# AdaLN block on one Trainium2 core: first batch's keys kept raw, scale in column blocks, keys and values by pairs, new engine orders

## What is computed

```
mod = (silu(c) @ wmod).reshape(4, 6, 1, 1024)          # sa, ca, ga, sb, cb, gb
ga, gb = sign * max(abs, 0.25)
h = layernorm(x) * (1 + ca) + sa
q, k, v = h @ Wqkv + bqkv                              # 3 x 256 columns
attn = softmax(q @ k.T / 16) @ v
x = x + ga * (attn @ Wo + bo)
h = layernorm(x) * (1 + cb) + sb
x = x + gb * (h @ weight.T + bias + LoRA(h))           # adapter by batch
```

## Time and profile before

| | us |
|---|---|
| median of 3 runs | 1043.1 (1042.88 to 1043.18) |
| the profiled execution | 1042.57, of which its span 1040.8 |
| PE busy | 1011.5 (97%) |
| VectorE busy | 663.6 (64%) |
| ScalarE busy | 309.2 (30%) |
| GpSimd busy | 231.2 (22%) |
| DMA | 180.74 MB, mean 174 GB/s |

### The profile page before, as it was taken

How to read it: one execution, slowest core, us unless ns; L and a number is a source line. 1 busy time by engine, 2 the same in 40 slices (tenths; PEclk the granted TensorE clock), 3 DMA queues, 4 the chain that set the end, 5 groups by cost and what they waited for, 6 DMA issues and landing times.

```text
span 1040.8 us, 12891 instructions
## 1 busy us (share of the span) xinstructions
PE 1011.5 (97%) x5158; PEld 831.6 (80%) x5158; DVE 663.6 (64%) x827; ACT 309.2 (30%) x460; POOL 231.2 (22%) x182
## 2 busy tenths in 40 slices
...
PEclk9899999999999999999999999999999999999999
...
GB/s 348 409 317 244 211 295 140 252 227 265 70 1 77 207 197 127 1 94 157 155 162 117 41 142 225 203 220 184 200 202 126 216 145 202 140 225 122 142 76 66
DMA packets 54475, 180.74 MB, mean 174 GB/s; under 512 B 5784, under 2 KB 6352, under 8 KB 54416
## 3 DMA queue, kind: packets, MB, share of 16 engines
...
q10 hardware_dynamic: 160, 0.53, 0.1%
...
## 4 chain that ended last, share of the span: by engine, by line
PE 91%; DMA 4%; DVE 2%; SPq 1%; issue 1%; POOL 0%; ACT 0%; DVEq 0%; POOLq 0%; ACTq 0%
PE pairC L1370 8%; PE pairA L1370 8%; PE pairC L1371 8%; PE pairC L1372 7%; PE pairA L1371 7%; PE pairA L1372 7%; PE pairD L1370 7%; PE pairD L1371 7%; PE pairD L1372 7%; PE pairB L1370 5%; PE pairB L1371 5%; PE pairB L1372 5%; DMA z_cols<-in_x_cols 2%; PE pairB L1526 1%; PE pairD L1478 1%; PE pairA L1478 1%
## 5 line engine op out<-in xcount | busy, mean ns | idle before, releaser
L923 POOL TENSOR_TENSOR xr<-xr,row_bc 128x1024 f32<-128x1024 f32 x32 | 79.9, 2503 | 110.1 <-DMA xr<-in_x 90.3
L936 POOL TENSOR_TENSOR res<-res,row_bc 128x1024 f32<-128x1024 f32 x32 | 81.7, 2565 | 83.4 <-DMA res<-x_dram 76.9
L1370 PE MATMUL pairC<-w_hi,h_hi 128*128 128x512 f32 (+1 forms) x256 | 90.1, 352 | 0.0
L1371 PE MATMUL pairC<-w_lo,h_hi 128*128 128x512 f32 (+1 forms) x256 | 90.0, 351 | 0.0
L1372 PE MATMUL pairC<-w_hi,h_lo 128*128 128x512 f32 (+1 forms) x256 | 89.6, 350 | 0.0
L1370 PE MATMUL pairD<-w_hi,h_hi 128*128 128x512 f32 (+1 forms) x224 | 77.6, 346 | 0.0
L1371 PE MATMUL pairD<-w_lo,h_hi 128*128 128x512 f32 (+1 forms) x224 | 77.6, 346 | 0.0
L1372 PE MATMUL pairD<-w_hi,h_lo 128*128 128x512 f32 (+1 forms) x224 | 77.2, 345 | 0.0
...
L1079 ACT ACTIVATE w_hi<-w_sum 128x1024 fp32r<-128x1024 f32 x32 | 33.8, 1059 | 100.5 <-DVE w_sum L1320 100.2
L1370 PE MATMUL pairB<-w_hi,h_hi 128*128 128x512 f32 (+1 forms) x160 | 59.8, 374 | 0.0
L1371 PE MATMUL pairB<-w_lo,h_hi 128*128 128x512 f32 (+1 forms) x160 | 59.3, 371 | 0.0
...
## 6 DMA issues: line engine op xcount, KB each, us to landing
wm<-in_wmod SPq DMA_DIRECT2D x48, 512.0 KB, 6.4
xr<-in_x SPq DMA_DIRECT2D x34, 512.0 KB, 4.0
z_cols<-in_x_cols SPq DMA_DIRECT2D x32, 512.0 KB, 6.3
x_dram<-xr POOLq DMA_DIRECT2D x32, 512.0 KB, 3.8
xs<-x_dram SPq DMA_DIRECT2D x32, 512.0 KB, 4.7
w2t<-in_w2t SPq DMA_DIRECT2D x32, 512.0 KB, 4.3
res<-x_dram SPq DMA_DIRECT2D x32, 512.0 KB, 5.7
out_y<-res POOLq DMA_DIRECT2D x31, 512.0 KB, 3.5
```

The lines of the kernel that those rows point to most:

```text
L923: nc.gpsimd.tensor_tensor(xt, xt, row_bc[:, :], ALU.add).then_inc(residual_made, 1)
L936: nc.gpsimd.tensor_tensor(rt, rt, row, ALU.add).then_inc(residual2_made, 1)
L1370: nc.tensor.matmul(out, left[0], right[0], start=first, stop=False)
L1371: nc.tensor.matmul(out, left[0], right[1], start=False, stop=False)
```

## The change

Everything in it is in the first batch, but for the five orders, which are new throughout.

- The scale (s = 0) is made in four blocks of 256 columns. A buffer now holds 256 columns of 512 rows of `wmod` (four pieces of 1 KB per partition where there was one of 4 KB), `M0(c)` multiplies two buffers, `MC0`, `MT0` and `MM0` finish two column tiles each, and `HH(0,0,k)` waits for block k alone.
- Mean and 1/deviation are spread apart (`BCM`, `BCP`), for both blocks of rows, and ScalarE copies them from PSUM to `bc` (`BMC`, `BPC`), from where `Z` reads. The way through DRAM is gone for block (0,1).
- `V0(c)` makes the first block's values two column tiles at a time, like `K0`.
- `KR` (ScalarE) copies the first batch's keys out of PSUM without bias into `k_raw`; `KH` and `KL` read from there later.
- The `wm` buffers beyond the first eight loads are 4, where there were 6 for loads 8 to 15 and 4 after.
- Keys' and values' weights come first: `PARTS` goes from (1,0), (1,1), (0,0), (0,1), (2,0), (2,1) to (1,0), (2,0), (1,1), (2,1), (0,0), (0,1).

```diff
-PARTS = ((1, 0), (1, 1), (0, 0), (0, 1), (2, 0), (2, 1))
+PARTS = ((1, 0), (2, 0), (1, 1), (2, 1), (0, 0), (0, 1))
...
 PE_ORDER = [
-    ("BCP", (), "A", None), ("M", (0, 0), "B", None), ("M", (0, 1), "B", None), ("M", (0, 2), "B", None),
...
 SP_ORDER = [
-    ("LN", 0, 0), ("LN", 0, 1), ("Lsm",), ("LN", 0, 2), ("LN", 0, 3), ("Lid",), ("LWq", 1, 0), ("LT", 0, 0, 0),
-    ("LT", 0, 0, 1), ("Lwm", 0, 0), ("Lwm", 0, 1), ("Lwm", 0, 2), ("Lwm", 0, 3), ("Lwm", 0, 4), ("Lwm", 0, 5),
...
+    ("LN", 0, 0), ("LN", 0, 1), ("Lsm",), ("LN", 0, 2), ("LN", 0, 3), ("Lid",), ("LT", 0, 0, 0), ("LWq", 1, 0),
+    ("Lwm", 0, 0), ("Lwm", 0, 1), ("LT", 0, 0, 1), ("Lwm", 0, 2), ("Lwm", 0, 3), ("LWq", 2, 0), ("LT", 0, 0, 2),
+    ("Lwm", 0, 4), ("Lwm", 0, 5), ("LWq", 1, 1), ("LT", 0, 0, 3), ("Lwm", 0, 6), ("Lwm", 0, 7), ("LWq", 2, 1),
+    ("LN", 0, 4), ("LN", 0, 5), ("LN", 0, 6), ("LN", 0, 7), ("LT", 0, 1, 0), ("LT", 0, 1, 1), ("LT", 0, 1, 2),
...
         def wm_slot(n):
-            return n if n < 8 else (n - 8) % 6 if n < 16 else n % 4
+            return n if n < 8 else n % 4
...
+            elif what == "K" and i[0] == 0:
+                eng.wait_ge(k_raw_made, 2 * i[1] + 2)
...
+                    if s == CA:
+
+                        half, at = k % 2, q * H + k // 2 * 2 * P
+                        src = wmod[half * BANK:(half + 1) * BANK, at:at + 2 * P].rearrange("(k p) n -> p k n", p=P)
+                        sp.dma_start(wm[k].rearrange("p (k n) -> p k n", k=4), src).then_inc(ld_wm[k], 16)
...
+                elif what == "KR":
+
+                    _, j, m = i
+                    act.wait_ge(k_done, 2 * j + m + 1)
+                    act.wait_ge(mod_used, 6)
+                    nc.scalar.activation(k_raw[:, m, j * CHUNK:(j + 1) * CHUNK], ps[:, m * BANK:(m + 1) * BANK],
+                                         ACT.Copy).then_inc(k_raw_made, 1)
...
-                    act.wait_ge(mod_made, 1)
+                    act.wait_ge(ca_made, k + 1 if b + j == 0 else 4)
...
+                elif what == "M0":
+
+                    c = i[0]
+                    if c == 0:
+                        pe.wait_ge(c_ready, 1)
+                    for k in range(CT):
+                        if k % 4 == 0:
+                            pe.wait_ge(ld_wm[2 * c + k // 4], 16)
+                        q = 32 * (k % 4)
+                        last = nc.tensor.matmul(ps[q:q + 32, 0:2 * P], scT[:, k * B:k * B + 32],
+                                                wm[2 * c + k // 4][:, k % 4 * 2 * P:(k % 4 + 1) * 2 * P],
+                                                start=(k < 4), stop=(k >= 4))
...
+                elif what == "V0":
+
+                    c = i[0]
+                    pe.wait_ge(w_lo_made, PARTS.index((2, c // 2)) + 1)
+                    pe.wait_ge(h0_lo_made, 2 * c + 2)
```

More of the change, by code:

```diff
@@ L709, in wait_emptied @@
             if what == "M":
-                eng.wait_ge(mod_made, i[0] + 1)
-            elif what == "BCP":
-                eng.wait_ge(z_made, 4)
+                eng.wait_ge(mod_made, i[0])
+            elif what == "M0":
+                eng.wait_ge(ca_made, i[0] + 1)
+            elif what == "BCM":
+                eng.wait_ge(spread_copied, 2 * i[0] + 2)
             elif what == "WU":
@@ L1229, in step @@
                     dve.wait_ge(hi_made, 4 * b + 2 * j + m + 1)
-                    nc.vector.scalar_tensor_tensor(lo[where], ps[:, m * BANK:(m + 1) * BANK],
+                    src = k_raw[where] if what == "KL" and b == 0 else ps[:, m * BANK:(m + 1) * BANK]
+                    nc.vector.scalar_tensor_tensor(lo[where], src,
                                                    bias_qkv[:, col + m, b:b + 1], hi[where].bitcast(F32),
@@ L1369, in product3 @@
             def product3(out, left, right, first, last):
-                nc.tensor.matmul(out, left[0], right[0], start=first, stop=False)
-                nc.tensor.matmul(out, left[0], right[1], start=False, stop=False)
-                return nc.tensor.matmul(out, left[1], right[0], start=False, stop=last)
+                nc.tensor.matmul(out, left[0], right[0], start=first, stop=False, skip_group_check=True)
+                nc.tensor.matmul(out, left[0], right[1], start=False, stop=False, skip_group_check=True)
+                return nc.tensor.matmul(out, left[1], right[0], start=False, stop=last, skip_group_check=True)
             def both(hi, lo, *where):
@@ L1405, in step @@
                     last.then_inc(mod_turned, 1)
-                elif what == "BCP":
+                elif what in ("BCM", "BCP"):
+                    j = i[0]
                     pe.wait_ge(ld_const, 16)
-                    pe.wait_ge(rstd_made, 1)
-                    for k in range(2):
-                        for t in range(4):
-                            at = k * CHUNK + t * P
-                            last = nc.tensor.matmul(ps[:, at:at + P], stat[:, 0, k, t:t + 1].to_broadcast([P, P]), ident,
-                                                    start=True, stop=True)
-                    last.then_inc(stat_spread, 1)
+                    if what == "BCM":
+                        pe.wait_ge(stat_made, 4 * j + 4)
+                    else:
+                        pe.wait_ge(rstd_made, j + 1)
+                    k = 0 if what == "BCM" else 1
+                    for t in range(4):
+                        at = k * CHUNK + t * P
+                        last = nc.tensor.matmul(ps[:, at:at + P], stat[:, j, k, t:t + 1].to_broadcast([P, P]), ident,
+                                                start=True, stop=True)
+                    last.then_inc(mean_spread if what == "BCM" else stat_spread, 1)
                 elif what == "RT0":
```

156 lines of the change are left out of this document (95 added, 61 removed), and 700 rows, old and new, of tables (ACT_ORDER, DVE_ORDER, PE_ORDER, POOL_ORDER).

## The result

The changed kernel takes **1047.35 us** (median of 5 runs, 1047.26 to 1050.09), the kernel before 1042.88 in the same comparison (5 runs, 1041.82 to 1043.18): a ratio of **1.0057, 95% interval 1.0045 to 1.0069**. It is slower by about 0.6%; I had forecast 1040.0, faster. The profiled span went from 1040.8 to 1045.6, +4.8.

What follows compares the result with a forecast made beforehand. PE, busy 97% of the span, was taken as the bound. The terms 0 - 1.5 - 0.3 - 1.0 + 0.5 - 0.8 = -3.1 us, from the median 1043.1, gave 1040.0 us, range 1037.0 to 1045.0.

Steps and rivals of the forecast that it cites:

- Part 3: Everything after the first batch's middle: same work, some waits of batch 3 closed, -0.8 us, from -1.2 to +2.
- Part 1: The head, up to `M(1,0)` near 50: keys start at 23.65 instead of 30.60, but the gain is paid back, 0.
- Part 2: First batch's middle: clock dip -1.5, holes -0.3, `wmod` wait -1.0, four buffers +0.5 us.
- Landing of the rows, 34.5: In the head, loads of rows 512 to 1023 of x start landing at 34.5 us, including 8e = 2.0.
- e: Extra cost of each narrow `wmod` load with 1 KB pieces in the head: 0.25 to 0.8 us, taken as 0.25.
- 5.35 + 1.28 n: Landing time in us after n loads of 512 KB at 409 GB/s, fitted to the kernel before.
- rival (a): Head: slow narrow loads delay the statistics; 1043.7 us at e = 0.8, 1047.5 at 1.28; 10% near 0.8, 10% slower.
- rival (b): The clock falls again in new gaps, at 38.9 to 44.5 or elsewhere: 1041.5 to 1042 us; 22% with other small waits.
- The term of +0.5 for four buffers: First batch's middle: `wmod` has four buffers throughout, so loads may come late; charged +0.5 us, from 0 to 2.
- a new order may open as many waits as it closes: After the first batch, over 1000 us of work: reason for the range -1.2 to +2 us around -0.8.
- (c): VectorE walk too slow, or `K0(0)` at full clock with e = 0, and all three later waits close: 1038 us; 7%.
- (d): Head: silu and statistics delay the first keys to where they were, `Z(0,0,0)` ending 7 us later; 1%.

Runs made afterwards that it cites:

- y1: The changed kernel run once more, unedited, on another chip: ratio 1.0043 to the kernel before.
- x4: The changed kernel with the eight scale loads in 4 KB pieces (scale made of other numbers, same work): 1043.07 us, ratio 1.0013 to the kernel before.
- y4: The changed kernel with `OL(3,1,1)` ahead of `PK(1)`, scale in 4 KB pieces, and unread filler matmuls ahead of `K0(0)` and `BCP(1)`: ratio 0.9998.
- x1: The changed kernel with one VectorE step moved, `OL(3,1,1)` ahead of `PK(1)`: 1045.2 us, ratio 1.0026 to the kernel before.
- w2_hold: The changed kernel with `OL(3,1,1)` ahead of `PK(1)`, 4 KB scale pieces, and VectorE held in the head until GpSimd made rstd: ratio 1.0006.
- w1_gate: The changed kernel in its own order, with GpSimd's residual add `RA(3,4)` held until `PK(1)` is done: ratio 1.0024 to the kernel before.
- w3: The changed kernel with `OL(3,1,1)` ahead of `PK(1)`, 4 KB scale pieces, and `M(1,1)`, `M(2,1)`, `M(4,0)`, `M(5,1)` each one step later: ratio 1.0103.
- v1: The changed kernel with `OL(3,1,1)` ahead of `PK(1)`, 4 KB scale pieces, and `M(1,2)`, `M(4,1)`, `M(5,2)` each one step earlier: ratio 1.0040.
- x2_spread: The changed kernel with `BCM(1)`, `BCP(1)` moved behind `K0(2)` on TensorE and `HH(0,0,3)` ahead of `BMC(1)` on ScalarE: ratio 1.0058.

## Why the prediction was wrong

The forecast was -3.1 us from the kernel before, the first profile has +4.8. Of the 7.9 between them the end of batch 3 and what follows (Part 3) are 3.7, the head (Part 1) 2.2 and the middle (Part 2) 1.9. In the second profile, +2.2, they are 1.2, 2.8 and 1.4. Of the signs of being wrong, those for `M(1,0)` (52.31), for the clock after 50 (0.50 at 628) and for the waits after 160 (2.7) came.

**Part 1, forecast 0, came to +2.2.** Most of the walk held. `K0(0)` started at 23.98 (23.65). A cold `K0(0)` cost nothing (y1). The chain behind it was VectorE's. The statistics ended at 41.17 (40.5). What failed, the largest last:

- *Landing of the rows, 34.5, was 35.38.* The term I had doubted, e, was about right: with pieces of 4 KB the statistics start at 32.83 to 33.85 (x4, y4), with 1 KB at 35.11 to 35.59, so eight loads cost 1.3 to 2.8 us, 0.16 to 0.35 each (I took 0.25); in x4 the statistics did not wait for their rows at all, so it may be more. The base, 5.35 + 1.28 n, gives 32.5 without e. The rule that I had weighed, of the Trainium skill, "DMA: Bandwidth & Descriptors", section Specifications (line rate from 512 B on), is not borne out here at 1 KB: 370 GB/s against 410 from 22 to 30 us. I wrote that e = 0 would give 1.4, which does not go with the slack of 2.7 us in rival (a); measured at equal clock it is 1.65 (`M(1,0)` in x1 and x4). x4 gains 3.5 there against the first profile, since its clock did not fall.
- *`BCP(1)` done by 44.5.* GpSimd's two instructions, 0.20 and 1.02 us when VectorE is idle, took 1.14 and 1.39, and `BCP(1)` itself 1.98 in place of 1.13. `V0(2)` was 1.15 late, 0.85 of it by `BCP(1)` at half clock; in x1_pk, with GpSimd just as slow but full clock, it was 0.13 late. I read GpSimd's durations from rows where the two engines did not meet; w2_hold shows what stretched them.
- *`V0(2)` in 2.8 us.* It took 3.76 in the first profile, 4.09 in the second, at half clock. That was rival (b), named with the right place (38.9 to 44.5) and a price of up to 2; it measured 0.9 to 1.3, plus 0.85 in `BCP(1)`. I had left it out of the sum, and it is 1.8 of the head's 2.2: without it (x1_pk) `M(1,0)` starts at 50.49, 0.4 behind the walk.

**Part 2, forecast -2.3, came to -1.4, then +1.1.** The dip at 84 us is gone, and the wait on `wmod` too, as forecast. The term of +0.5 for four buffers showed as no wait in the two profiles of the changed kernel, but as 1.0 and 1.8 us of waiting weight loads in x1_pk and w1_gate, with the same steps up to there and `M(1,0)` to `S(0,0)` 0.5 and 1.1 us longer. w3 and v1 show how little slack is left: a few steps one place either way cost 4 to 10 us. `S(0,0)` at 128.88 is 3.6 past the 125.3 of the list, of which 2.2 are the head. What I had no term for is `S(0,0)` to `S(1,0)`, +1.08: before had two places where two `M` stand together, the change puts each of `M(5,0)` to `M(5,3)` alone, and two `RT0` ahead of four-step groups of turns. The gaps can be read off the trace (0.10 to 0.32 a place, 0.42 before `O(0,0)`), one place was tested (0.24 for a pair); their sum as the cause is argued, not shown.

**Part 3, forecast -0.8, came to +2.9 in the first profile, +0.4 in the second.** The step that failed is "a new order may open as many waits as it closes", which I had put at -1.2 to +2 and then taken at its good end. The order opened one wait, at `O(3,4)`, worth 3.4 with the clock behind it, and its place could be seen beforehand: `PK(1)`, which waits for TensorE, stood ahead of the step that TensorE asks for next. Its size could not: with the same order the wait was 1.82, 0.47, 0.32 (x2_spread) and 2.42 us (x4_wide), by how GpSimd's adds fell. Where the step was moved or the add held, and `PK(1)` was short, `PV(2,1,1)` to the first `F` is 154.4 to 154.55 against 155.10, or -0.6: close to the -0.8. The feed-forward part was 390.25 us in before, 390.2 to 392.0 in the versions; what makes this spread I leave open.

**Rivals.** (a) is false at its price (e was near 0.25, not 0.8). (b) is true, in the head and again at 628 us. (c) did not come. (d) is false. None named the wait at the end of batch 3, and the range of Part 3, to +2, was too narrow for the first profile. One reading of the rows was loose: in the earlier trace rows the clock is under 9 only in slice two, while the first and the last slice are low in busy time.
